# First layer's mixture of experts: every expert on every token, replaced by token rows sorted by expert in 127 tiles

## The chip, the cores and the metric

The program runs on one core of one Trainium2 chip (trn2). The metric is the device time of one execution in microseconds (us), all four layers included.

## The reference

A four-layer network on 1,024 tokens (16 sequences of 64) of width 256. Each layer does cross-attention to a context of 1,601 rows, self-attention, and a feed-forward part, each added to x. Only the feed-forward part of the first layer is changed. It is a mixture of 64 experts, of which each token uses 8, and one shared expert:

```
def _mlp(x, gw, uw, dw):
    return jax.nn.silu(x @ gw.T) * (x @ uw.T) @ dw.T
x = hidden_states.reshape(B * S, H)              # 1024 x 256, after a layer norm
rw = _route(x, gate_w, gate_bias)                # 1024 x 64, 8 nonzero weights in a row
expert_out = jax.vmap(lambda gw_, uw_, dw_: _mlp(x, gw_, uw_, dw_))(Wg, Wu, Wd)   # hidden width 176
routed = jnp.einsum('eth,te->th', expert_out, rw)
shared = _mlp(x, Sg, Su, Sd)                     # hidden width 352
out = (routed + shared).reshape(B, S, H)
```

All is float32. `_route` takes, for each token, the 4 best of 8 groups of experts and the 8 best experts in these.

## The kernel before

The program is a chain of stages. A stage (`stage`) gives each engine its own list of instructions, with semaphores between them, and ends with all engines meeting (line 44). Of the stages only these matter here.

`cross_attention` of layer 0 loads the context in pieces of 800.5 KB from SyncE's queue (line 440), two batches ahead.

`refresh` (tag nf0) adds the output of self-attention to x and makes the normed rows, turned into `net.xnT` (features on partitions, tokens along the row).

`route_groups` makes the routing weights `score` (tokens on partitions, 8 tiles of 64) on VectorE, a chain in which each step waits for the one before. Line 1390 is its last step. TensorE then turns them (line 1341), and VectorE copies them to `rwT` (line 1393).

`gated_experts` computes every expert on all 1,024 tokens. The hidden rows of all experts stand in 91 tiles of 128 (3 of the shared expert, 88 of the 64 routed ones), each with its gate, up and down weights (`e_w`, 384 KB). A tile is done in two units of 512 tokens. Each product is written as three float32r products of high and low parts (`split_product`, line 1458), so a unit has 18 matmuls of 512 columns: 6 for gate, 6 for up, 6 for down. ScalarE and VectorE split the weights and the hidden values into those parts. The down products of all 182 units are summed in the accumulators of PSUM. At the end the sum is turned and added to x (line 1529). The next stage, `refresh` nx1, begins with line 283 on VectorE.

`top1_experts`, the third layer's mixture (14 experts, 1 for each token), already works on sorted rows. It counts the tokens of each expert, gives each its place in 21 tiles of 128 rows, scatters the rows to `x_rows` in HBM by 8 indirect transfers of GpSimd (line 1638; 128 rows of 1 KB each), loads them back (line 1766), and takes each tile with its expert's weights (1,154 KB, line 1629, six slots): 2 transposes (line 1652), 8 matmuls of 128 columns (line 1664), 4 matmuls of 256 columns (line 1674), all plain float32. The trace has two records for each plain float32 matmul and one for each transpose. Each tile's output goes to `y_rows` (line 1625). When all are there, 8 indirect transfers (line 1642) bring the rows back into token order and line 1755 adds them.

## Time and profile before

| what | value |
|---|---|
| median of 3 runs | 4831.44 us (4830.58 to 4834.53) |
| the profiled execution: time, span | 4833.99 us, 4832.2 us |
| TensorE busy | 4280.3 us, 89% of the span |
| VectorE, ScalarE, GpSimd busy | 2477.3, 1964.5, 556.7 us |
| mean granted TensorE clock | 0.937 of 2.4 GHz |
| routing and experts of layer 0 | 919.5 to 1713.0 us of the span |
| moved by DMA | 223.20 MB, 46 GB/s over the span |

The busy shares are means over stages that differ. For this change the place to read is the stretch between line 1390 and the next stage's line 283. In the listing of instructions in order of time, a row gives start, duration, engine, line, operation, what it writes and reads, the count of instructions merged into the row, and in brackets how long the engine was idle before it and who ended that. A merged row's duration runs from its first start to its last end.

### The profile page before, as it was taken

The numbers are of one execution on the slowest core, as the hardware profiler recorded it, in microseconds if no ns is written. First come the engines' busy times: TensorE is split into PE (matmuls) and PEld (weight loads), VectorE is DVE, ScalarE is ACT, GpSimd is POOL, SyncE is SP. The second block draws the span as 40 slices with busy tenths as digits, with TensorE's granted clock in tenths as the row PEclk, the third lists the DMA queues.
The fourth block names the chain that finished last, engine by engine and source line by source line (L and its number), as shares of the span: only waits on it lengthen the run. The fifth ranks groups of instructions, "written<-read, shape, count | busy, mean of one in ns | idle before, by whom it ended". The sixth has DMA issues, their size and how long they took to land. (4 is left out here: it accounts for less than half of the span.)

```text
span 4832.2 us, 144528 instructions
## 1 busy us (share of the span) xinstructions
PE 4280.3 (89%) x65816; PEld 3416.8 (71%) x65816; DVE 2477.3 (51%) x4205; ACT 1964.5 (41%) x3848; POOL 556.7 (12%) x264
## 2 busy tenths in 40 slices
PE   7999996599999979999987689999973769999988
PEld 5877774488888858888863557787752648888865
DVE  4555553556666655555535535555534145555532
ACT  3545442233333334444532235454532234444431
POOL 1111111000000011111104001111102011111100
PEclk9999998599999989999988799999986889999988
DMA  2111100021111111111103011111110721111100
GB/s 70 43 37 40 39 23 17 19 80 48 48 50 50 46 56 38 41 42 38 38 24 84 19 41 41 43 37 43 37 19 10 283 67 38 45 38 38 38 10 31
DMA packets 89805, 223.20 MB, mean 46 GB/s; under 512 B 28880, under 2 KB 52576, under 8 KB 86480
## 3 DMA queue, kind: packets, MB, share of 16 engines
q1 hardware_dynamic: 85696, 209.13, 13.7%
q8 instruction: 521, 8.54, 0.7%
q10 hardware_dynamic: 2736, 2.75, 0.2%
q0 software_dynamic: 768, 2.10, 0.1%
q14 instruction: 84, 0.69, 0.1%
HBM read 196.23 MB, written 9.32 MB: 43 GB/s over the span
## 5 line engine op out<-in xcount | busy, mean ns | idle before, releaser
L647 DVE TENSOR_REDUCE x_pm<-banks 128x4 f32<-128x1536 f32 (+2 forms) x512 | 935.6, 1827 | 690.2 <-PE banks L548 690.2
L749 ACT ACTIVATE x_pl<-banks 128x384 f32<-128x384 f32 x1536 | 628.8, 497 | 710.2 <-PE banks L531 710.2
L473 POOL TENSOR_TENSOR x_cl<-xnT,x_ch 128x1601 fp32r<-128x1601 f32 x116 | 386.1, 3328 | 2176.7 <-ACT x_ch L764 2176.7
L754 ACT ACTIVATE x_kT<-banks,x_bk 128x384 f32<-128x384 f32 (+2 forms) x512 | 305.5, 597 | 537.4 <-PE banks L559 537.4
L571 PE MATMUL banks<-x_wh,x_ch 128*128 128x256 f32 (+1 forms) x1664 | 489.9, 294 | 0.0
L531 PE MATMUL banks<-x_q,x_kT 32*128 32x128 f32 x13312 | 483.0, 276 | 3.1 <-issue 2.9
L548 PE MATMUL banks<-x_kT,x_q 32*128 32x384 f32 (+2 forms) x4096 | 458.5, 512 | 14.0 <-DVE x_v L679 9.0
L571 PE MATMUL banks<-x_wh,x_cl 128*128 128x256 f32 (+1 forms) x1664 | 468.6, 282 | 0.0
L571 PE MATMUL banks<-x_wl,x_ch 128*128 128x256 f32 (+1 forms) x1664 | 466.9, 281 | 0.0
L559 PE MATMUL banks<-x_ch,x_wh 128*128 128x384 f32 (+2 forms) x1024 | 410.4, 401 | 44.2 <-DVE x_cl L730 43.1
L531 PEld LDWEIGHTS banks<-x_q,x_kT 32*128 32x128 f32 x13312 | 436.5, 185 | 7.0 <-issue 4.4
L679 DVE TENSOR_TENSOR x_v<-banks,x_bv 128x256 f32<-128x256 f32 (+1 forms) x832 | 316.8, 419 | 196.3 <-PE banks L571 196.3
L559 PEld LDWEIGHTS banks<-x_ch,x_wh 128*128 128x128 f32 x1024 | 194.2, 190 | 292.4 <-ACT x_pl L749 210.3
L749 ACT ACTIVATE x_pe<-banks 128x512 f32<-128x512 f32 x512 | 264.4, 602 | 292.5 <-PE banks L531 292.5
L580 PE MATMUL banks<-x_pl,x_v 128*32 128x64 f32 x18432 | 325.2, 222 | 49.4 <-issue 48.8
L559 PE MATMUL banks<-x_ch,x_wl 128*128 128x384 f32 (+2 forms) x1024 | 358.1, 350 | 0.0
L559 PE MATMUL banks<-x_cl,x_wh 128*128 128x384 f32 (+2 forms) x1024 | 357.8, 349 | 0.2 <-issue 0.2
L580 PEld LDWEIGHTS banks<-x_pl,x_v 128*32 128x32 f32 x18432 | 289.9, 112 | 54.6 <-issue 54.0
L571 PEld LDWEIGHTS banks<-x_wh,x_ch 128*128 128x128 f32 (+1 forms) x1664 | 307.9, 185 | 6.7
L571 PEld LDWEIGHTS banks<-x_wh,x_cl 128*128 128x128 f32 (+1 forms) x1664 | 308.1, 185 | 0.2
L571 PEld LDWEIGHTS banks<-x_wl,x_ch 128*128 128x128 f32 (+1 forms) x1664 | 307.4, 185 | 0.0
L666 DVE TENSOR_SCALAR x_num<-banks,parity 128x64 f32<-128x64 f32 x128 | 36.3, 284 | 523.3 <-PE banks L580 523.3
(345 smaller groups left out, 6964.2 us busy)
## 6 DMA issues: line engine op xcount, KB each, us to landing
xnT<-in_ctxT SPq DMA_DIRECT2D x120, 800.5 KB, 4.4
e_w<-in_L_pack SPq DMA_DIRECT2D x91, 384.0 KB, 3.1
e_w<-in_L_pack SPq DMA_DIRECT2D x21, 1154.0 KB, 7.6
a_swap<-a_raw SPq DMA_DIRECT2D x64, 128.0 KB, 2.3
actT<-in_ctxT SPq DMA_DIRECT2D x8, 800.5 KB, 4.9
e_rw<-routed_rows SPq DMA_DIRECT2D x64, 64.0 KB, 2.9
x_rows<-e_zero SPq DMA_DIRECT2D x1, 2688.0 KB, 9.6
e_xt<-x_rows ACTq DMA_DIRECT2D x3, 896.0 KB, 10.3
```

Of the source, the lines that this page charges most:

```text
L473: nc.gpsimd.tensor_tensor(cl[:, u, k, 0:CTX], staged(b, k), ch[:, u, k, 0:CTX], ALU.subtract).then_inc(low_done, 1)
L531: last = nc.tensor.matmul(sets[g % 2][j][0:n, (t - lo) * P:(t - lo + 1) * P], kT[r, c, t * P:t * P + n], qb[r, u, c], start=False, stop=Tr ...
L548: last = nc.tensor.matmul(into[j][:, 0:hi - lo], qb[r, u, c], kT[r, c, lo:hi], start=not masked, stop=True, skip_group_check=masked)
L559: last = nc.tensor.matmul(bank[:, 0:hi - lo], w[:, 0, k, c * P:(c + 1) * P], x[:, u, k, lo:hi], start=(k == n == 0), stop=(k == KC - 1 and ...
L571: last = nc.tensor.matmul(bank[0:w, (t - lo) * D:(t - lo + 1) * D], x[:, u, k, t * P:t * P + w], y[:, 1, k, :], start=(k == m == 0), stop= ...
L580: last = nc.tensor.matmul(bank[32 * j:32 * j + 32, e * S:(e + 1) * S], v[0:w, u, t, at:at + 32], probabilities(c, j, t, t + 1)[0:w, 0, e * ...
L647: nc.vector.tensor_reduce(pm[:, c, :, g], src[:, :, 0:hi - lo], AX.X, ALU.max).then_inc(max_done, 1)
L666: nc.vector.tensor_scalar(num[:, c], src, own, None, ALU.mult).then_inc(o_taken, 1)
L679: ins = nc.vector.tensor_tensor(heads, bank[0:w, (t - lo) * D:(t - lo + 1) * D].rearrange("p (h e f) -> p h e f", e=2, f=16), bvb[0:w].rea ...
L749: nc.scalar.activation(probabilities(c, j, lo, hi).rearrange("p t q -> p (t q)"), mine[j][:, 0:(hi - lo) * P], ACT.Exp).then_inc(exp_done, 1)
L754: nc.scalar.activation(kT[:, c, lo:hi], mine[1 if g == 0 and inside(b if c else b - 1) else 0][:, 0:hi - lo], ACT.Identity, bias=col[:, c: ...
```

## The change

`gated_experts` goes, with its high and low parts, and `routed_experts` comes in its place. The 8 x 1,024 pairs of token and expert are sorted by expert into 127 tiles of 128 rows (each expert begins a new tile, and 127 is the most that can be needed; all 127 are always computed). A tile takes its expert's weights in two transfers whose address comes from a register: gate and up, 128 rows of 2,816 bytes (360,448 bytes), and down, 88 rows of 2,048 bytes (180,224 bytes). Five slots hold them. The shared expert is 16 units on tokens in their own order, with weights that are loaded once. A unit has plain float32 matmuls: 2 of 352 columns for gate and up, 2 transposes of the hidden values, 2 matmuls of 256 columns for down; a routed one has 2 transposes of its rows besides. The rows are scattered by 64 indirect transfers and fetched back by 64, each of 128 rows of 1 KB. Sorted rows are loaded 8 tiles at a time (1,024 KB) and outputs stored 4 tiles at a time (512 KB). The HBM buffer of the sorted rows is cleared in 8 transfers of up to 2 MB during layer 0's cross-attention. `route_groups` no longer turns the weights. The diff, cut to its core:

```diff
+                if clear is not None and b < CLEARS:
+                    rows = clear[b * CLEAR_TILES * P:min(b * CLEAR_TILES + CLEAR_TILES, ROUTED_TILES) * P, :]
+                    rows = rows.rearrange("(j p) n -> p j n", p=P)
+                    sp.dma_start(rows, spread(net.zero[:].unsqueeze(1), (P, rows.shape[1], D))).then_inc(net.cleared, 16)
...
-def gated_experts(net, tag, packed, rwT, rw_rows):
...
+def routed_experts(net, tag, xn, score, mask, x_rows, y_rows):
...
+    E, K = 64, 8
+    GU, HID = 352, 88
+    WIDTH = KC * GU + 2 * D
+    SLOTS = 5
+    LOAD, X_RING = 8, 3
+    STORE, Y_RING = 4, 2
+    RING = 16
+    SHARED = 2 * TILES
+    UNITS = SHARED + ROUTED_TILES
+    LOADS = -(-ROUTED_TILES // LOAD)
+    STORES = -(-ROUTED_TILES // STORE)
...
+        def weights(n):
+            return ws[:, n % 2] if n < SHARED else w[:, (n - SHARED) % SLOTS]
...
 
         @block.sync
         def _(sp):
+            def load_rows(n):
+                tiles = tiles_of(n, LOAD)
+                rows = x_rows[tiles.start * P:tiles.stop * P, :].rearrange("(j p) n -> p j n", p=P)
+                sp.dma_start(xt[:, n % X_RING, 0:len(tiles)], rows).then_inc(x_in[n % X_RING], 16)
+            def load_weights(j):
+                e = sp.value_load(owner_i[0:1, j:j + 1], min_val=0, max_val=E - 1)
+                slot_w = w[:, j % SLOTS]
+                sp.dma_start(slot_w[:, 0:KC * GU], d["L0_pack"][bass.ds(e, 1)].rearrange("o p n -> p (o n)")).then_inc(w_in[j % SLOTS], 16)
+                sp.dma_start(slot_w[0:HID, KC * GU:], d["L0_down"][bass.ds(e, 1)].rearrange("o p n -> p (o n)")).then_inc(w_in[j % SLOTS], 16)
+            sp.dma_start(before[:], d["before"]).then_inc(const_in, 16)
+            sp.dma_start(const[:], d["sort_rows"]).then_inc(const_in, 16)
+            sp.dma_start(ws[:], d["L0_shared"].rearrange("s p n -> p s n")).then_inc(shared_in, 16)
+            sp.wait_ge(tiles_known, 1)
+            for j in range(SLOTS):
+                load_weights(j)
+            sp.wait_ge(scattered, 16 * TILES * K)
+            for n in range(X_RING):
+                load_rows(n)
+            for j in range(ROUTED_TILES):
+                sp.wait_ge(y_ready, j + 1)
+                if j + SLOTS < ROUTED_TILES:
+                    load_weights(j + SLOTS)
+                if j % LOAD == 0 and j and j // LOAD + X_RING - 1 < LOADS:
+                    load_rows(j // LOAD + X_RING - 1)
+                n = j // STORE
+                tiles = tiles_of(n, STORE)
+                if j == tiles.stop - 1:
+                    rows = y_rows[tiles.start * P:tiles.stop * P, :].rearrange("(j p) n -> p j n", p=P)
+                    sp.dma_start(rows, y[:, n % Y_RING, 0:len(tiles)]).then_inc(stored[n % Y_RING], 16)
+            for s in range(Y_RING):
+                sp.wait_ge(stored[s], 16 * ((STORES - s + 1) // Y_RING))
+        @block.gpsimd
+        def _(pool):
+            pool.wait_ge(net.cleared, 16 * CLEARS)
+            pool.wait_ge(slots_known, 1)
+            for n in range(TILES * K):
+                pool.indirect_dma_start(x_rows, bass.IndirectOffsetOnAxis(ap=slot_i[:, n:n + 1], axis=0), xn[:, n // K, :],
+                                        None).then_inc(scattered, 16)
+            for s in range(Y_RING):
+                pool.wait_ge(stored[s], 16 * ((STORES - s + 1) // Y_RING))
+            for n in range(TILES * K):
+                if n >= RING:
+                    pool.wait_ge(added, n - RING + 1)
+                pool.indirect_dma_start(yt[:, n % RING, :], None, y_rows,
+                                        bass.IndirectOffsetOnAxis(ap=slot_i[:, n:n + 1], axis=0)).then_inc(back[n % RING], 16)
...
+            def turn(n):
+                j = n - SHARED
+                load = j // LOAD
+                pe.wait_ge(x_in[load % X_RING], 16 * (load // X_RING + 1))
+                if j >= 2:
+                    pe.wait_ge(xT_ready, j - 1)
+                for c in range(KC):
+                    last = nc.tensor.transpose(x_ps[j % 2][:, c * P:(c + 1) * P], xt[:, load % X_RING, j % LOAD, c * P:(c + 1) * P],
+                                               net.ident[:])
+                last.then_inc(turned, 1)
+            def gate_up(n):
+                j = n - SHARED
+                if j >= 0:
+                    pe.wait_ge(w_in[j % SLOTS], 32 * (j // SLOTS + 1))
+                    pe.wait_ge(xT_ready, j + 1)
+                if n >= 2:
+                    pe.wait_ge(h_ready, n - 1)
+                for k in range(KC):
+                    x = net.xnT[:, k, (n // 2) * P:(n // 2 + 1) * P] if j < 0 else xT[:, j % 2, k]
+                    last = nc.tensor.matmul(gu_ps[n % 2][:, 0:GU], x, weights(n)[:, k * GU:(k + 1) * GU], start=(k == 0),
+                                            stop=(k == KC - 1))
+                last.then_inc(gu_full, 1)
+            def turn_hidden(n):
+                pe.wait_ge(h_ready, n + 1)
+                if n >= 2:
+                    pe.wait_ge(hT_ready, n - 1)
+                for i in range(2):
+                    last = nc.tensor.transpose(h_ps[n % 2][0:HID, i * P:(i + 1) * P], h[:, n % 2, i * HID:(i + 1) * HID], net.ident[:])
+                last.then_inc(h_turned, 1)
...
             def down(n):
+                o = output(n)
+                first, final = n >= SHARED or n % 2 == 0, n >= SHARED or n % 2 == 1
+                pe.wait_ge(hT_ready, n + 1)
+                if first and 2 <= o:
+                    if o - 2 < TILES:
+                        pe.wait_ge(shared_added, o - 1)
+                    else:
+                        pe.wait_ge(y_ready, o - 1 - TILES)
+                for i in range(2):
+                    at = KC * GU + i * D
+                    last = nc.tensor.matmul(y_ps[o % 2][:, 0:D], hT[:, n % 2, i], weights(n)[0:HID, at:at + D],
+                                            start=(first and i == 0), stop=(final and i == 1))
                 last.then_inc(down_done, 1)
...
+            pe.wait_ge(const_in, 32)
+            flat = mask[:].rearrange("p t e -> p (t e)")
+            nc.tensor.matmul(cum, before[:], flat, start=True, stop=True)
+            nc.tensor.matmul(count, net.ones[:], flat, start=True, stop=True).then_inc(counted, 1)
+            pe.wait_ge(owner_ready, 1)
+            nc.tensor.matmul(count[0:1, 0:P], owner[:], net.ident[:], start=True, stop=True).then_inc(owner_turned, 1)
+            pe.wait_ge(shared_in, 16)
+            for n in range(-3, UNITS):
+                if n + 3 == SHARED:
+                    pe.wait_ge(slots_known, 1)
+                    pe.wait_ge(tiles_known, 1)
+                if SHARED <= n + 3 < UNITS:
+                    turn(n + 3)
+                if 0 <= n + 2 < UNITS:
+                    gate_up(n + 2)
+                if 0 <= n + 1 < UNITS:
+                    turn_hidden(n + 1)
+                if n >= 0:
+                    down(n)
...
+            for t in range(TILES):
+                link(nc.vector.tensor_tensor(pre[:, t + 1], pre[:, t], count[:, t * E:(t + 1) * E], ALU.add))
...
+            def take_rows(n):
+                j = n - SHARED
+                dve.wait_ge(turned, j + 1)
+                if j >= 2:
+                    dve.wait_ge(gu_full, n - 1)
+                nc.vector.tensor_copy(xT[:, j % 2], x_ps[j % 2][:, 0:D].rearrange("p (c n) -> p c n", c=KC)).then_inc(xT_ready, 1)
+            def multiply(n):
+                dve.wait_ge(silu_done, n + 1)
+                if n >= 2:
+                    dve.wait_ge(h_turned, n - 1)
+                nc.vector.tensor_tensor(h[:, n % 2], g[:, n % 2], gu_ps[n % 2][:, 2 * HID:GU], ALU.mult).then_inc(h_ready, 1)
+            def take_output(n):
+                o = output(n)
+                dve.wait_ge(down_done, n + 1)
+                if n < SHARED:
+                    nc.vector.tensor_tensor(net.x[:, o], net.x[:, o], y_ps[o % 2][:, 0:D], ALU.add).then_inc(shared_added, 1)
+                    return
+                j = n - SHARED
+                s = j // STORE
+                if s >= Y_RING:
+                    dve.wait_ge(stored[s % Y_RING], 16 * (s // Y_RING))
+                nc.vector.tensor_copy(y[:, s % Y_RING, j % STORE], y_ps[o % 2][:, 0:D]).then_inc(y_ready, 1)
...
+            for n in range(-3, UNITS):
+                if SHARED <= n + 3 < UNITS:
+                    if n + 3 == SHARED:
+                        for t in range(TILES):
+                            find_weights(t)
+                    take_rows(n + 3)
+                if 0 <= n + 2 < UNITS:
+                    multiply(n + 2)
+                if n >= 0 and (n >= SHARED or n % 2):
+                    take_output(n)
...
+            for n in range(TILES * K):
+                t, k = n // K, n % K
+                dve.wait_ge(back[n % RING], 16 * (n // RING + 1))
+                if k:
+                    dve.wait_ge(added, n)
+                nc.vector.scalar_tensor_tensor(net.x[:, t, :], yt[:, n % RING, :], weight[:, t, k:k + 1], net.x[:, t, :], ALU.mult,
+                                               ALU.add).then_inc(added, 1)
...
+            def silu(n):
+                act.wait_ge(gu_full, n + 1)
+                if n >= 2:
+                    act.wait_ge(h_ready, n - 1)
+                nc.scalar.activation(g[:, n % 2], gu_ps[n % 2][:, 0:2 * HID], ACT.Silu).then_inc(silu_done, 1)
+            def take_hidden(n):
+                act.wait_ge(h_turned, n + 1)
+                if n >= 2:
+                    act.wait_ge(down_done, n - 1)
+                nc.scalar.activation(hT[:, n % 2].rearrange("p i n -> p (i n)"), h_ps[n % 2][0:HID, 0:2 * P], ACT.Copy).then_inc(hT_ready, 1)
+            for n in range(-3, UNITS):
+                if 0 <= n + 2 < UNITS:
+                    silu(n + 2)
+                if 0 <= n + 1 < UNITS:
+                    take_hidden(n + 1)
...
+ROUTED_TILES = (TOK * 8 + 64 * (P - 1)) // P
+CLEAR_TILES = 16
+CLEARS = -(-ROUTED_TILES // CLEAR_TILES)
...
+    o["L0_pack"], o["L0_down"] = (np.ascontiguousarray(m) for m in (routed[:, :, :704], routed[:, :88, 704:]))
```

`find_weights`, not shown, is three VectorE instructions of 512 elements for each of 8 token tiles. Between `need` and the first unit VectorE does some 25 further short steps on 64 to 512 elements, chained as those of `route_groups` are.

## Rows read from the trace of the kernel before

**Rows 1.** The page, busy time by engine.

```profile
PE 4280.3 (89%) x65816; PEld 3416.8 (71%) x65816; DVE 2477.3 (51%) x4205; ACT 1964.5 (41%) x3848; POOL 556.7 (12%) x264
```

**Rows 2.** Busy time in a stretch of `gated_experts`: length, engines, granted clock, DMA share, GB/s.

```profile
1300.00:1500.00 200.00, 200.00 (x884) 165.62 (x883) 125.50 (x172) 75.84 (x123) 0.00 (x0) 1.00 0.16 48
```

**Rows 3.** In order of time: both edges of the stretch that changes.

```profile
950.26 0.43 DVE L1390 TENSOR_SCALAR r_score<-r_score 128x512 f32<-128x512 f32 x1
...
954.88 0.80 SPq L1441 DMA_DIRECT2D e_w<-in_L_pack  x2
...
1713.05 0.43 DVE L283 BATCH_NORM_STATS2 nx_stats<-x_tok 128x6 f32<-128x256 f32 x1 [1.09 <-PEq L44]
```

**Rows 4.** In order of time: chained VectorE steps of `route_groups`.

```profile
939.89 2.04 DVE L1299 TENSOR_TENSOR r_eq<-r_eq,r_tri 128x64 f32<-128x64 f32 x8
...
942.69 0.69 DVE L1302 TENSOR_REDUCE r_rank<-r_gt 128x64 f32<-128x512 f32 x1
```

**Rows 5.** In order of time: one tile of `top1_experts` on TensorE.

```profile
3801.27 0.38 PE L1652 MATMUL banks<-ident,e_xt 128*128 128x128 f32 x2
...
3801.49 1.95 PE L1664 MATMUL banks<-e_xT,e_w 128*128 128x128 f32 x16
...
3803.28 1.89 PE L1674 MATMUL banks<-e_w,e_h 128*128 128x256 f32 x8
...
3805.01 0.38 PE L1652 MATMUL banks<-ident,e_xt 128*128 128x128 f32 x2
```

**Rows 6.** In order of time: first and last of 8 scatters.

```profile
3760.18 0.17 DVE L1735 CAST e_sloti<-e_slot 128x8 int32<-128x8 f32 x1
...
3761.25 1.21 POOL L1638 DMA_INDIRECT x_rows<-nf_xn,e_sloti  x1 [16.61 <-DVE e_sloti L1735]
...
3770.38 0.96 POOL L1638 DMA_INDIRECT x_rows<-nf_xn,e_sloti  x1 [0.31 <-issue]
```

**Rows 7.** In order of time: last output, first and last of 8 gathers, last addition.

```profile
3866.46 0.42 DVE L1751 TENSOR_TENSOR e_y<-banks,e_w 128x256 f32<-128x256 f32 x1 [1.30 <-PE banks L1674]
3868.88 0.97 POOL L1642 DMA_INDIRECT e_yt<-y_rows,e_sloti  x1 [97.54 <-DMA y_rows<-e_y]
...
3877.69 0.95 POOL L1642 DMA_INDIRECT e_yt<-y_rows,e_sloti  x1 [0.31 <-issue]
...
3880.50 0.48 DVE L1755 SCALAR_TENSOR_TENSOR x_tok<-e_yt,e_weight,x_tok 128x256 f32<-128x256 f32 x1 [0.78 <-DMA e_yt<-y_rows,e_sloti]
```

**Rows 8.** In order of time: SyncE's queue in `top1_experts`, six weight loads, later a steady tile.

```profile
3760.20 6.43 SPq L1629 DMA_DIRECT2D e_w<-in_L_pack  x6
...
3798.19 0.33 SPq L1625 DMA_DIRECT2D y_rows<-e_y  x1
3799.27 0.34 SPq L1629 DMA_DIRECT2D e_w<-in_L_pack  x1
```

**Rows 9.** Transfers by what they move: count, KB each, median us from issue to landing.

```profile
e_w<-in_L_pack SPq DMA_DIRECT2D x91, 384.0 KB, 3.1
...
a_w<-in_L_q SPq DMA_DIRECT2D x1, 1024.0 KB, 5.0
a_w<-in_L_k SPq DMA_DIRECT2D x1, 1024.0 KB, 7.9
...
e_yt<-y_rows,e_sloti POOLq DMA_INDIRECT x8, 2.8
```

**Rows 10.** In order of time: four context loads of layer 0.

```profile
67.29 62.77 SPq L440 DMA_DIRECT2D xnT<-in_ctxT  x4
```

**Rows 11.** Busy time in stretches of 4 and 2 us where weights, then sorted rows, are loaded.

```profile
3774.00:3778.00 4.00, 0.00 (x0) 0.00 (x0) 0.00 (x0) 0.00 (x0) 0.00 (x0) 0.50 1.02 427
...
3787.00:3789.00 2.00, 2.00 (x11) 2.00 (x11) 0.00 (x0) 0.00 (x0) 0.00 (x0) 0.50 1.11 350
```

**Rows 12.** Busy time around line 252 of `refresh` na0, granted clock third from last.

```profile
760.00:764.00 4.00, 0.48 (x3) 0.35 (x3) 1.36 (x3) 0.05 (x1) 0.03 (x1) 0.80 0.01 4
764.00:768.00 4.00, 4.00 (x10) 3.15 (x11) 1.26 (x4) 1.73 (x3) 4.00 (x6) 0.50 0.01 2
768.00:770.00 2.00, 2.00 (x8) 1.64 (x7) 1.62 (x8) 0.29 (x1) 1.55 (x3) 0.69 0.00 0
```

More of the change, by code:

```diff
@@ L1302, in rank_below, with route_groups @@
     link(nc.vector.tensor_reduce(rank, gt.rearrange("p t i j -> p (t i) j"), AX.X, ALU.add))
-def route_groups(net, tag, rwT):
+def route_groups(net, tag, score, left):
     nc, d = net.nc, net.dram
     E, G, K = 64, 8, 8
-    with ExitStack() as mem, stage(nc, "w_in logits sig chain rw_ready turned ones_set") as (
-            block, w_in, logits, sig, chain, rw_ready, turned, ones_set):
+    with ExitStack() as mem, stage(nc, "w_in logits sig chain rw_ready") as (
+            block, w_in, logits, sig, chain, rw_ready):
         w = net.sb(tag + "_gw", [P, KC, E], ctx=mem)
@@ L1454, in _ @@
         @block.tensor
         def _(pe):
-            def split_product(out, u, at, right, start, stop):
-                for m, (a, b) in enumerate(((wh, 0), (wl, 0), (wh, 1))):
-                    last = nc.tensor.matmul(out, a[:, u, at:at + P], right[b], start=start and m == 0,
-                                            stop=stop and m == 2, skip_group_check=not start and not stop)
-                return last
-            def down(n):
-                u, half = n // 2 % 2, n % 2
-                pe.wait_ge(h_lo, n + 1)
-                for c in range(KC):
-                    last = split_product(acc[c][half], u, o_d + c * P, (hh[:, n % 2], hl[:, n % 2]), n < 2, n >= UNITS - 2)
-                last.then_inc(down_done, 1)
@@ L1486, in _ @@
-            down(UNITS - 1)
-            for half in range(2):
-                pe.wait_ge(out_ready[half], 2)
-                for t in range(4 * half, 4 * half + 4):
-                    for c in range(KC):
-                        last = nc.tensor.transpose(net.ps[half][:, (t % 4) * D + c * P:(t % 4) * D + (c + 1) * P],
-                                                   out_sb[:, c, t * P:(t + 1) * P], net.ident[:])
-                last.then_inc(turned, 1)
+            def turn(n):
[8 more added lines that the diff above has]
+                last.then_inc(turned, 1)
@@ new lines, in _ @@
+            dve.wait_ge(const_in, 32)
+            link(nc.vector.tensor_tensor(steps[:], spread(pre[:, TILES].unsqueeze(2), (P, E, 8)),
+                                         spread(edges.unsqueeze(1), (P, E, 8)), ALU.is_gt))
+            link(nc.vector.tensor_reduce(need[:], steps[:], AX.X, ALU.add))
+            link(nc.vector.tensor_copy(sums[:, 0, E:], need[:]))
+            for s in range(6):
+                a, b = sums[:, s % 2], sums[:, 1 - s % 2]
+                link(nc.vector.tensor_tensor(b[:, E:], a[:, E:], a[:, E - (1 << s):2 * E - (1 << s)], ALU.add))
@@ L1533, in _ @@
+            dve.wait_ge(added, TILES * K)
         @block.scalar
         def _(act):
-            def split_high(tile):
-                u = tile % 2
-                act.wait_ge(w_in[u], 16 * (tile // 2 + 1))
-                nc.scalar.activation(wh[:, u], w[:, u], ACT.Copy).then_inc(w_hi, 1)
-            for half in range(2):
-                tok = slice(half * HALF, (half + 1) * HALF)
-                nc.scalar.activation(xh[:, :, tok], net.xnT[:, :, tok], ACT.Copy).then_inc(x_hi, 1)
-            split_high(0)
```

243 lines of the change are left out of this document (99 added, 144 removed).

## The prediction

> **What bounds the kernel now.** I read the page first: TensorE is busy for 89% of the span [rows 1]. A share over all stages does not price a change in one, so I went to the order of time at the edges of the stretch that changes [rows 3]: the routing weights are ready at 950.7 us (950.26 + 0.43) and the next stage's first VectorE step starts at 1713.05. These 762.4 us are what is replaced. A window in the middle [rows 2] shows TensorE busy for all of 200 us at the full clock with 884 matmul records, 0.226 us each. A unit has 18, so it takes 4.07 us, and 182 units take 741 us. DMA is at a share of 0.16 and VectorE at 0.63, so nothing but TensorE sets the pace, and what counts is how much time the new stage's TensorE, its transfers and its serial parts need.
>
> **TensorE per sorted tile.** `top1_experts` has the same kinds of instruction at the full clock [rows 5]. Two transposes start at 3801.27 and the next group at 3801.49: 0.22 us. Sixteen records of 128 columns take 1.79 us (to 3803.28), 0.112 each. Eight records of 256 columns take 1.73 us (to 3805.01), 0.216 each. A record thus costs about 0.004 us beside its columns, and one of 352 columns comes to 0.297. A sorted tile has four of these for gate and up (1.19 us), four of 256 for down (0.86) and two pairs of transposes (0.44): 2.49 us. 127 tiles are 316 us. Three units of the shared expert are unfinished when the first sorted rows are awaited (the loop turns rows three units ahead): one gate/up, two hidden turns, three downs, 1.19 + 0.44 + 2.6 = 4.2 us.
>
> **The serial part in front.** I keep to the clock of the span.
> - `route_groups` no longer turns and copies the weights. With a stage change of 1.1 us (the idle time in the last row of [rows 3]) the new stage issues its first transfer at 951.8, where before it was 954.9 [rows 3].
> - The constants land some 3.1 us later, as 384 KB do [rows 9]: 955.
> - Two count matmuls of 512 columns, four records, at half clock (four times 0.112, doubled, each): 3.5 us, 958.5.
> - The VectorE chain to the slots: some 20 short steps of 0.255 us (2.04 over 8), five on 512 elements at 0.72 (0.69 with a small gap) [rows 4], and eight maxima at 0.14 or so, estimated between those: 9.8 us, 968.3. The first scatter starts 1.07 us after its slots' step starts [rows 6]: 969.2.
> - 64 scatters. Eight took 9.13 us from first start to last start [rows 6], 1.30 each, so 63 intervals are 82 us: 1051.2. The last lands 2.8 us later, as a gather does [rows 9], and the first load of sorted rows (1,024 KB) takes 5.0 us [rows 9] and 0.3 of waking: 1059.3.
>
> Under these 90 us lie the shared expert's 16 units (2.27 us each, 36 us, and a few more at half clock), the three steps of `find_weights` per token tile (24 steps of 0.7, 17 us) and the first five weight loads (6 loads took 6.4 us to issue [rows 8]). They cost nothing, for the scatters last longer than all of them.
>
> **The tail.** After the last down: 0.42 us of copy and 2.0 us until the first gather [rows 7], and 0.8 for a last store three times the size: 3.2 us. 64 gathers at 1.26 us (8.81 over 7) and 3.3 us from the last one's start to the end of the last addition (3880.50 + 0.48) [rows 7]: 82.6 us. VectorE's additions stay hidden, 0.48 in each 1.26. Stage change 1.1 us.
>
> **The sum without stalls.** 1059.3 + 316.2 + 4.2 + 2.6 (TensorE comes from idleness and runs about 5 us at half clock, as after the gap in [rows 12]) + 3.2 + 82.6 + 1.1 = 1469.2. Against 1713.05 that is 243.8 us less. The profiled execution took 4833.99 us, of which 4832.2 are span, so 4590.2; it stands 2.5 us above the median shown, which makes 4588.
>
> **Other engines in the loop.** VectorE has two copies of 256 elements and a product of 176 per tile, about 0.42 + 0.42 + 0.33, ScalarE about 0.7: below 2.49. SyncE loads a value, issues two weight transfers, and a store every fourth and a row load every eighth tile. One load with its value takes 1.22 us (6.43 less 0.34, over 5) [rows 8]. The second transfer lies between 0.45 (a plain issue with its gap) and 1.22. I take 0.5; with stores and row loads 1.9 us per tile, at most 2.6.
>
> **The eight clears.** 2 MB each at 350 GB/s [rows 11] are 6 us of transfer, behind a context load. These loads come 20.8 us apart (62.77 less the issue, over 3) [rows 10], and DMA is mostly idle there, so each clear is over before the next load. Nothing; were every clear to delay a load that something waits for, up to 6 us each, 48 in all.
>
> **The transfers, where I expect the stalls.** Bytes per tile: weights 541 KB, output 131 KB, sorted rows 131 KB. With 9.2 KB rows the trace shows 427 GB/s, with 1 KB rows 350 [rows 11]. I take 380 for the weights and 350 for the rest: 1.42 + 0.37 + 0.37 = 2.2 us (bounds 1.9 and 2.3), below 2.49, so the mean rate does. The timing is tighter. The load for tile j+5 is released by tile j's output copy, 0.5 us after its down, and gate/up of j+5 comes two tiles and one pair of transposes after that down: 4.98 + 0.22 - 0.5 = 4.7 us. It needs 0.75 us until the issue (3798.52 to 3799.27) [rows 8], 3.1 us for 384 KB [rows 9] and 0.4 for the other 147 KB, 4.3 in all with the second issue. The slack is 0.35 us. Loads queue in order: of two loads of 1,024 KB issued 0.45 us apart the second lands 2.9 us later by its own issue, 3.35 in all [rows 9]. So a load of sorted rows holds the queue for 3.0 to 3.35 us, say 3.2, and a store of 512 KB for 1.5. The weights of the next tile are issued 2.49 us after those before, and find 1.42 + 3.2 - 2.49 = 2.1 us in front of them, and 0.4 from the store just before (1.42 + 1.5 - 2.49). Less the slack that is 2.2 us of TensorE stall at each of the 13 row loads in the loop: 29 us. Stores by themselves give 0.1 each, 1 or 2 us. In a busy queue every landing will be a little later; it goes round a loop of five tiles, so 0.3 us more is 0.06 per tile, 7 us. Together 37: **4588 + 37 = 4625 us**.
>
> **A rule on the 88 rows.** The Trainium skill, "DMA: Bandwidth & Descriptors", section on why a DMA increments its semaphore by 16, says that a transfer is spread over the largest number of engines up to 16 that divides its slowest dimension; for 88 rows that is 11. No transfer of this trace shows it. It is the second rival below.
>
> **The rivals.**
> 1. All transfers covered. For it: the mean need is 2.2 of 2.49 us, and in `top1_experts` a greater one never stalled TensorE. Against it: there six slots gave several times the lead. 4588, to 4600. Chance 0.15.
> 2. Down weights on 11 of the 16 DMA engines. These then move 55,296 bytes per tile (8 rows each of 2,816, 2,048, 1,024 and 1,024), at 380/16 GB/s 2.33 us, at 350/16 2.53, which is just over 2.49. The weights take 1.64 us, the slack falls to 0.1, a row load costs 2.9 us (13 times, 38), a store 0.5 (16 times, 8), and landings as above or a little worse 10: 4588 + 56 = 4644, to 4660. Chance 0.22.
> 3. The clock. After 4 us with TensorE busy for 0.48 it ran at 0.50, which is 1.2 GHz, until about 769 [rows 12]. If each of the 13 stalls brings that, half of 5 us is lost each time: 34 us more, 4660, with rival 2 4680. Against it: that gap followed a stretch with TensorE busy 0.48 of 4 us, mine follow 15 us of full work. Chance 0.13.
> 4. SyncE: with 1.22 us for the second transfer it needs 2.6 us per tile. The load's way also grows by 0.7. 127 times 0.11 and the stalls: 4640 to 4660. Chance 0.05.
> 5. Slower than before: the indirect transfers. The trace has only 8 in a row. If a queue of them holds no more than eight and each further one waits for an earlier one to land and be taken up, the interval is no longer 1.3 us. 112 of the 128 are beyond the eighth, and 206 us of forecast gain divided by them is 1.84, so the side changes at an interval of 3.1 us. At 4 us the kernel takes 4930. For it: nothing in the trace but that it ends at eight. Against it: landings of 2.8 us are longer than the interval, so at least two are in flight without a pause. Chance 0.05.
> 6. The forecast, 4600 to 4640: 0.40.
>
> **How the numbers follow.** The forecast is 4625. The range goes from 4586, with all covered, to 4700, which takes in rivals 2, 3 and 4, and 2 with 3 and the upper bounds of the loads; what is left out is rival 5 and worse queues than these, some 0.1. About 0.2% (10 us) is what a measurement can tell from no change. All cases but rival 5 are faster: 0.94. The same, 0.01: an interval of the indirect transfers just at 3.1. Slower 0.05.
>
> **What the profile after would show.** Right: records of 352 columns 0.30 us apart; 127 tiles in 350 to 360 us, with TensorE waiting for `w_in` (weights) once in eight tiles for about 2 us, one tile after each row load; two runs of 64 indirect transfers of 80 us with TensorE idle, 52 us or so in the first; layer 0's cross-attention unchanged. Wrong: waits for weights at every tile (rival 2, or a slower queue), the granted clock under 1 in the loop (3), SyncE issuing without waiting (4), intervals of POOL over 1.3 us (5), or a steady 2.49 us (1).

## The result, and the profile after

Changed kernel: 4763.06 us median of 4 runs (4757.26 to 4770.7). Kernel before, beside it: 4832.98 us. The ratio is 0.9854, 95% interval 0.9837 to 0.9871: faster by some 70 us, where I had forecast 4625 us and a range of 4586 to 4700. The same kernel run again later (`a_again`) gave 0.985. The direction was right; of the 206 us of gain that were forecast, some 70 came.

The page of the changed kernel, busy time by engine, answers to [rows 1]:

```profile
PE 3955.9 (83%) x64206; PEld 3096.3 (65%) x64206; DVE 2213.9 (47%) x4094; ACT 1766.6 (37%) x3675; POOL 679.0 (14%) x392
```

TensorE lost 324 us of work, the span only 77. The instructions in order of time, at the places of [rows 3], [rows 6] and [rows 7]:

```profile
984.68 0.33 SPq L1469 DMA_DIRECT2D e_before<-in_before  x1
...
1105.45 0.68 DVE L1641 TENSOR_TENSOR e_eq<-e_spot,e_slot 128x512 f32<-128x512 f32 x1
...
1558.70 0.98 POOL L1504 DMA_INDIRECT e_yt<-routed_y,e_sloti  x1 [476.61 <-DMA routed_y<-e_y]
...
1640.35 0.48 DVE L1663 SCALAR_TENSOR_TENSOR x_tok<-e_yt,e_weight,x_tok 128x256 f32<-128x256 f32 x1 [0.78 <-DMA e_yt<-routed_y,e_sloti]
1644.87 0.43 DVE L286 BATCH_NORM_STATS2 nx_stats<-x_tok 128x6 f32<-128x256 f32 x1 [4.04 <-PEq L40]
```

With the stalls, the forecast put the next stage at 1469.2 + 37 = 1506.2; it starts at 1644.87, 138.7 later. Place by place:

| term | forecast | measured | late by |
|---|---|---|---|
| stage's first transfer | 951.8 | 984.7 | 32.9 |
| from there to the first sorted turn | 107.5 | 121.0 | 13.5 |
| first sorted turn to its gate/up | 0.2 | 16.6 | 16.4 |
| 127 tiles, first gate/up to the last down's end | 359.8 | 432.5 | 72.7 |
| tail, gathers, stage change | 86.9 | 90.1 | 3.2 |

Three places make nearly all of it: the clears (priced at nothing), the shared expert and `find_weights` beside the scatters (priced at nothing, 13.5 + 16.4 us), and the loop (its stalls priced too low). In the loop the waits of TensorE, from 1122 to 1545 us, are:

```profile
PE banks L1529 <- DMA e_w<-in_L_down: 69.1, 41, 6.0
PE banks L1529 <- issue: 13.7, 1, 13.7
```

69 us in 41 waits for weights, where I had 37 in all. The second row is the first sorted tile waiting for VectorE's `find_weights`. A load of sorted rows (in short, a row load) and what it does, in order of time:

```profile
1184.51 0.39 SPq L1461 DMA_DIRECT2D e_xt<-routed_x  x1
...
1185.84 0.34 SPq L1466 DMA_DIRECT2D e_w<-in_L_pack  x1
...
1187.60 1.45 PE L1529 MATMUL banks<-e_w,e_xT 128*128 128x352 f32 x4 [0.74 <-DMA e_w<-in_L_down]
...
1195.60 2.71 PE L1529 MATMUL banks<-e_w,e_xT 128*128 128x352 f32 x4 [5.25 <-DMA e_w<-in_L_down]
```

And the same place as busy time (third from last: granted clock), answering to [rows 2] and [rows 12]:

```profile
1194.00:1200.00 6.00, 4.40 (x10) 2.97 (x11) 0.34 (x1) 0.70 (x2) 0.00 (x0) 0.52 0.56 179
...
1422.00:1522.00 100.00, 85.19 (x356) 59.88 (x355) 32.75 (x89) 17.73 (x58) 0.00 (x0) 0.91 0.72 221
```

The mechanism of the forecast is there. The tile whose weights were issued just ahead of the row load waits 0.74 us, and the tile whose weights were issued behind it (at 1185.84) waits 5.25: 6.0 us here, where I had 2.2. Over the 13 row loads of the loop these pairs of waits add up to 61.6 of the 69 us, 4.7 us for each. The landing events of the trace show that a transfer does not land at one moment: the 16 parts of this row load land from 1190.2 to 1193.0, those of the weights behind it from 1191.2 to 1195.56, and the matmuls start at 1195.60, with the last part. After the long wait the clock is granted at half, 1.2 GHz, for some 5 us: the tile's four records of 352 columns take 2.71 us instead of 1.35. A tile without a wait takes 2.49 us, as priced.

The clears, around the first one. TensorE in order of time, then the DMA queues in 92 to 96 us (packets, MB, share of 16 engines):

```profile
92.56 0.58 PE L587 MATMUL banks<-x_pe,x_v 128*32 128x64 f32 x25
95.96 0.33 PE L587 MATMUL banks<-x_pe,x_v 128*32 128x64 f32 x4 [2.82 <-issue]
```

```profile
q1 hardware_dynamic: 1478, 1.51, 106.8%
q8 instruction: 1, 0.02, 1.5%
```

TensorE stops for 2.8 us in the middle of a group of 32 matmuls, where the program has no wait, while the clear holds all DMA engines and one 16 KB packet of instructions is under way among its packets. From 96 to 102 us the clock is at half. In the traces of the changed kernel, of `a_again` and of `e2` (below) I count 30 gaps over 1.2 us in TensorE's work between 60 and 430 us, and each of the 30 has such a packet in it or ending at most 0.2 us before it. The packet itself takes no longer than in quiet stretches (0.96 us here), so that it was late because it stood behind the clear is inferred.

Last, the shared expert's units beside the scatters, ScalarE in order of time:

```profile
1008.78 0.32 ACT L1673 ACTIVATE e_g<-banks 128x176 f32<-128x176 f32 x1 [1.67 <-issue]
...
1060.42 0.32 ACT L1673 ACTIVATE e_g<-banks 128x176 f32<-128x176 f32 x1 [22.02 <-DMA nx_bq<-in_L_xattn_bq]
...
1088.43 0.32 ACT L1673 ACTIVATE e_g<-banks 128x176 f32<-128x176 f32 x1 [22.02 <-DMA nx_bq<-in_L_xattn_bq]
```

Until 1012 us a unit takes 2.27 us, as forecast. Then four units take 77 us, until some 5 us after the scatters are through; the transfer named as releaser was over long before. Each time it is a result of TensorE that reaches ScalarE or VectorE late (up to 17.5 us behind the recorded end), while what ScalarE and VectorE hand on arrives at once.

### The profile page after: what moved, and what is told of

The parts are those of the page before. It is cut to its first block and busy times, and to the rows that moved or that the text cites. A ratio compares the mean times of both kernels' runs of the same rounds, so it can differ in the third digit from the quotient of the medians.

```text
span 4755.4 us, 142721 instructions
## 1 busy us (share of the span) xinstructions
PE 3955.9 (83%) x64206; PEld 3096.3 (65%) x64206; DVE 2213.9 (47%) x4094; ACT 1766.6 (37%) x3675; POOL 679.0 (14%) x392
## 6 DMA issues: line engine op xcount, KB each, us to landing
routed_x<-zero SPq DMA_DIRECT2D x7, 2048.0 KB, 11.5
```

## The experiments

All start from the changed kernel. "Loop" is the time from the first sorted gate/up to the start of the last down record, "start" the stage's first transfer, "to tile 0" from there to the first sorted gate/up.

| run | ratio to before | start | to tile 0 | loop |
|---|---|---|---|---|
| changed kernel | 0.9854 | 984.7 | 137.6 | 432.1 |
| `a_again` | 0.985 | 979.6 | 139.5 | 434.1 |
| `e2_small_clears` | 0.9908 | 1005.9 | 135.8 | 437.9 |
| `e3_weights_first` | 0.9834 | 981.1 | 126.7 | 427.6 |
| `e4_scatter_after_units` | one run, 4756.81 us | 980.4 | 139.6 | 430.7 |
| `s8_slots8` | 0.9662 | 973.5 | 136.3 | 346.5 |
| `c_clears_in_self_attention` | 0.9717 | 945.1 | 111.0 | 435.8 |
| `l2_load2` | 0.9682 | 981.4 | 107.8 | 392.8 |
| `d8_down_128rows` | 0.9558 | 978.5 | 110.9 | 317.6 |
| `o8_one_transfer` | 0.9562 | 974.8 | 111.4 | 317.6 |
| `d5_down_128rows` | 0.9782 | 975.6 | 137.7 | 400.6 |
| `r5_down_80_and_8` | 0.9864 | 972.4 | 137.8 | 436.7 |
| `x8_down_96rows` | 0.9658 | 977.9 | 138.3 | 337.8 |
| `m_clears_between` | 1.0008 | 1047.3 | 139.3 | 438.7 |
| `n_clears_midway` | 0.9782 | 949.5 | 135.9 | 425.4 |
| `b_best` | 0.953 | 947.0 | 130.5 | 317.5 |

The intervals of the ratios are 0.001 to 0.0023 to either side; the other columns come from one profiled execution each. How far these scatter is seen in kernels that do not differ at the place: the start in 11 kernels with the eight clears of 2 MB is 972.4 to 984.7, the loop in 8 kernels that leave it alone 425.4 to 438.7. Four kernels (`c`, `l2`, `d8`, `o8`) ran together on one chip, and there "to tile 0" is 111.4 us or less; on three other chips, and in the first profile of the changed kernel, it is 126 or more. So kernels on different chips are compared by their columns, and by ratio only on the same chip.

**The clears.** Smaller ones first, one behind each context load:

```diff
-CLEAR_TILES = 16
+CLEAR_TILES = 5
                     load_context(b + 2, k)
+                    n = KC * b + k
+                    if clear is not None and n < CLEARS:
+                        rows = ...
```

> The same 16.3 MB of zeros, but in 26 transfers of 640 KB, one behind each context load, in place of 8 of 2 MB. Theory A (a 2 MB transfer fills the DMA engines for 6 us; the one instruction fetch that falls into it comes late, TensorE stands for 3 us in the middle of a group and then runs at half clock for 5 to 6 us, some 4 us lost at each clear): a 640 KB transfer lasts under 2 us, the fetch is hardly late, and the first transfer of the sorted stage comes at 952 to 960 us instead of 984.68, the whole kernel at 4732 to 4740 us. Rival B (every byte of a clear costs the same, by plain contention): no change within 5 us.

Neither came: the stage starts at 1005.9, some 28 us later than with the 2 MB clears. TensorE's unexplained waits in 60 to 420 us (total, times, longest) for this kernel, and then for the changed one (`a_again`):

```profile
PEld banks L588 <- issue: 32.3, 28, 3.8
PE banks L588 <- issue: 24.5, 14, 3.6
```

```profile
PEld banks L587 <- issue: 22.4, 23, 2.4
PE banks L587 <- issue: 15.9, 9, 2.3
```

The kernel before has 6.2 us in 5. The gaps have not gone. A clear right behind a context load is one burst with it. The size and the time from issue to landing of a clear in the changed kernel, in `e2`, and in `n_clears_midway` (below), where it lies alone:

```profile
routed_x<-zero SPq DMA_DIRECT2D x7, 2048.0 KB, 11.5
routed_x<-zero SPq DMA_DIRECT2D x25, 640.0 KB, 7.1
routed_x<-zero SPq DMA_DIRECT2D x25, 640.0 KB, 3.3
```

The extra time comes from their number. ScalarE takes up the 19th piece of context at 428.8 us in the kernel without clears in this stage (`c`, next), at 466.2 in the changed one, which has then done all eight of its clears, and at 468.0 in `e2`, which has done 17 of 26; the 29th piece at 645.7, 683.7 and 705.2. So a small clear behind a load costs 2.3 us and a large one 4.1 to 4.7, and there are three times as many. Moved out of the stage (in `attend_pairs`, one behind each of its eight steps):

```diff
+            if extra_bias == "alibi":
+                for n in range(CLEARS):
+                    sp.wait_ge(biased, n + 1)
+                    rows = net.to_clear[...]
+                    sp.dma_start(rows, spread(net.zero[:].unsqueeze(1), ...)).then_inc(net.cleared, 16)
```

> The eight clears of 2 MB issued in layer 0's self-attention instead, one for each of its eight pairs of batches, some 9 us apart, where VectorE sets the pace and TensorE issues a tenth of the instructions. Theory A (in the cross-attention a clear holds up an instruction fetch of TensorE and costs the clock): the cross-attention ends as in the kernel before, nothing waits in the self-attention, and the kernel gains 25 to 35 us on the changed one, a ratio to the kernel before of 0.978 to 0.980. Rival B (the clears cost the same wherever they lie): 0.985 as the changed kernel.

The start is at 945.1: the clears' whole cost is gone, 33 us against the mean of 978 of the eleven kernels that have them unchanged. (The forecast's 951.8 was itself 6.7 us late, and the first profile's 984.7 is the latest of the eleven.) The rest of its ratio, under the 0.978 expected, goes with the chip ("to tile 0"). To tell the burst from the count, the small clears were put between the loads, with `sp.wait_ge(s_full, CYCLES * b + 4 * k + 7)` ahead of each:

> The 26 clears of 640 KB again in the cross-attention, but issued midway between two context loads rather than right behind one, where they made the kernel 28 us slower than the 2 MB clears did. Theory A2 (a burst costs when it lasts longer than TensorE can go without its next instruction fetch, and a small clear right behind a context load made 26 long bursts): alone, each lasts 2 us, less than a context load's 2.3, and the sorted stage starts at 945 to 955 us. Rival B2 (each transfer of zeros in this stage costs 1 to 1.5 us wherever it lies): the stage starts at 985 us or later.

The slowest of all (4832.85 us, the time of the kernel before), so this run does not decide between the two; and it is not the clears that make it slow: SyncE stood in that wait when the next context load was due, and ScalarE waited for it:

```profile
ACT x_ch L773 <- DMA xnT<-in_ctxT: 51.6, 13, 5.4
```

TensorE's gaps in mid-group were gone. With `4 * k + 2` in place of `4 * k + 7`, so that SyncE is free again in time:

> The 26 clears of 640 KB once more, now behind the second and sixth of a batch's eight score groups, some 8 us after a context load is due, so that SyncE is free again before the next load is. In the run before, the wait stood until the seventh group, SyncE came late to every second context load (15 us late, ScalarE waited 4 us for each of 13), and the stage began at 1047 us; but TensorE's unexplained gaps in the middle of groups were gone. Theory A2 (length of the burst decides): no such gaps (under 7 us in 60 to 420 us, as in the kernel before, against 16 with 2 MB clears and 24 with small ones behind the loads), no late load, and the sorted stage starts at 943 to 957 us. Rival B2 (each transfer costs wherever it lies): 975 us or later.

```profile
PEld banks L589 <- issue: 11.7, 21, 1.8
...
PE banks L589 <- issue: 5.0, 5, 1.7
```

The start is at 949.5 and the gaps are those of the kernel before: the same bytes in as many transfers, where they lie alone, leave the start 4.4 us behind that of `c`, which is within the scatter of the starts. Rival B2 is out, and theory A2 has its numbers. What stays untested is whether it is the length of the burst or that a write stands right behind a load.

**The shared expert and `find_weights`.** All eight calls of `find_weights` ahead of VectorE's loop over the units:

> The 24 steps of find_weights moved ahead of VectorE's loop over the units. Theory: they stand exposed behind the shared expert's units (1105.4 to 1121.8 us), so moved under the scatters they cost nothing and the kernel gains 14 to 17 us, to about 4747. Rival: the shared expert's units start 17 us later, their stalls move with them, and the end of the stage stays where it is (0 to 3 us).

"To tile 0" falls by 11 to 13 us against the changed kernel and by 9 to 10 against `e2` and `s8` on the same chip: more than half of the 16.4, for the units' backlog then shows. The ratio is 0.002 lower, which lies within the two intervals. GpSimd made to wait for the units:

```diff
             pool.wait_ge(slots_known, 1)
+            pool.wait_ge(shared_added, TILES - 2)
```

> GpSimd waits for six of the eight additions of the shared expert before its first scatter, so that units and scatters no longer lie side by side. Theory C (running indirect scatters hold up TensorE's completions): the units run at 2.27 us each throughout, all but three are done within 36 us of the slots, also beside the first five weight loads; the kernel is 20 to 25 us slower than the changed one, since nothing is hidden. Rival D (the units are held up by the first five weight loads, which keep the DMA engines full, and what follows is their backlog): the units stall here as well, from some 10 us after the weight loads start.

One run only. Busy time from 1000 to 1020 us, with weight loads and no scatter:

```profile
1000.00:1020.00 20.00, 20.00 (x90) 14.79 (x89) 4.74 (x14) 5.39 (x18) 0.00 (x0) 1.00 0.38 110
```

Rival D is out: the units run at full pace beside the loads. The expected loss of 20 to 25 us did not come: tile 0 comes no later than in the changed kernel, since the hiding had failed there anyway. And on one chip four kernels show no hold-up at all; here `d8` with units, scatters and weight loads together, 997 to 1030 us:

```profile
997.00:1030.00 33.00, 29.25 (x130) 21.19 (x128) 10.90 (x26) 7.79 (x27) 25.07 (x27) 1.00 0.70 252
```

> The changed kernel once more, unaltered, as the control of this group. In its first profile, and in those of three kernels of the first group (small clears, find_weights first, eight slots), the shared expert's units were held up between the scatters; in the four kernels of the second group they were not, though nothing there touches this place. If that belongs to the kernel, the hold-up is seen here as well and find_weights starts 120 us behind the stage's first transfer; if it belongs to the chip or the execution, it can be absent, with find_weights 46 us behind the first transfer and a ratio to the kernel before near 0.979 in place of 0.985.

The unaltered kernel shows the hold-up again (139.5). By `e4` it needs running scatters, and it is absent in the four profiles from one chip and present in the other profiles with scatters beside the units. Why TensorE's results are late then, and why not there, stays open.

**The loop.** Three more slots, `SLOTS = 8`:

> Eight weight slots in place of five. Theory L (the stalls are bursts: the row loads and stores hold the queue for 3 us and the lead is only 4.7 us of time): with three more tiles of lead, 7.5 us, the waits for the weights go to under 10 us of 69, the granted clock in the loop to 0.98 or more, and the kernel to 4680 to 4700 us. Rival R (the DMA engines cannot carry a tile's bytes in 2.49 us, whether by bytes or because 88 rows use only some of the engines): the waits stay nearly as they are, 4745 to 4760 us.

The loop falls from about 432 to 346.5 us and the ratio to 0.9662 (4660.78 us, better than the 4680 expected), with the clock at 0.98; but 17.7 us of waits in 11 are left, not under 10. So both theories have a part: the lead was most of it, and rival R's rate is what remains (below). Then the row loads in small pieces, `LOAD, X_RING = 2, 9`:

> Five slots, the sorted rows loaded two tiles (256 KB) at a time instead of eight (1 MB). Theory L (the stalls come from the bursts, each row load holding the queue for 3 us against a lead of 4.7 us): most of the waits for weights go, from 69 to under 25 us, and the ratio is 0.972 to 0.977. Rival (the lead is too short for the weights' own way in a busy queue, bursts or not): the waits stay above 50 us and the ratio above 0.981.

Loop 392.8 with waits of 47.3 us in 57, longest 2.6: between what the theory (under 25) and the rival (over 50) had said; the ratio, 0.9682, is helped by the chip. Small pieces bring half of what eight slots bring (43 us against `c` on the same chip). The rest is not the bursts: five slots are short even for the weights' own way. For what remained, the down weights were padded:

```diff
-    (routed[:, :, :704], routed[:, :88, 704:])
+    (routed[:, :, :704], routed[:, :, 704:])
-                sp.dma_start(slot_w[0:HID, KC * GU:], d["L0_down"]...
+                sp.dma_start(slot_w[:, KC * GU:], d["L0_down"]...
```

> Eight slots, and the down weights fetched as 128 rows (40 of them zeros), still in a transfer of their own. If 88 rows keep only 11 of 16 DMA engines at work, the fullest engine carries the same bytes as before (8 rows), so nothing changes: within 5 us of the kernel with eight slots alone (ratio 0.9662). If bytes count, 82 KB more per tile at 289 GB/s are 0.28 us, 127 times: up to 36 us more, less what was slack, so 0.970 to 0.974.

> Eight slots, and a tile's weights in one transfer of 128 rows of 4,864 bytes, as the kernel before packs them: this part of the change undone. By bytes it carries as much as the kernel with 128 down rows, 0.970 to 0.974 of before; if longer rows run faster (427 against 350 GB/s for the longest and the 1 KB rows in the trace of before) it gets some of it back, 0.965 to 0.968; if the two transfers cost something of their own (the second issue, a second landing), it is faster than the kernel with eight slots, under 0.965.

Neither "nothing" nor "slower": with 15% more weight bytes the loop falls from 346.5 to 317.6 us, 127 tiles at 2.49, without a wait. With one transfer it is the same, but both run at TensorE's own pace, so a small difference between them would not show. Busy time from 1150 to 1350 us for eight slots with 88 rows, and with 128:

```profile
1150.00:1350.00 200.00, 185.42 (x866) 135.15 (x865) 78.98 (x218) 43.23 (x144) 0.00 (x0) 0.98 0.96 289
```

```profile
1150.00:1350.00 200.00, 200.00 (x965) 148.11 (x964) 87.64 (x240) 48.14 (x161) 0.00 (x0) 1.00 1.00 358
```

At a share of 0.96 the queue moves 289 GB/s, which is 301 for a full share; with 128 rows 358. A tile's 803 KB (weights 541, rows and output 262) take 2.67 us at 301 GB/s, more than TensorE's 2.49; the 885 KB with padding take 2.47 at 358. So the rate of the queue binds the kernel with 88 rows even with eight slots: 346.5 us over 127 tiles is 2.73. The DMA counts for the same stretch (under 512 B are the completions, the small packets that end a transfer):

```profile
DMA packets 36248, 57.84 MB, mean 289 GB/s; under 512 B 2369, under 2 KB 20719, under 8 KB 36230
```

```profile
DMA packets 44454, 71.66 MB, mean 358 GB/s; under 512 B 3069, under 2 KB 23796, under 8 KB 44433
```

The packets of 2 to 8 KB are the weights, 216 a tile in the first kernel and 256 in the second. That is 71.8 and 80.6 tiles, and 33.0 and 38.1 completions per tile. With 16 for the gate and up weights, 4 for a quarter of a store and 2 for an eighth of a row load, 11.0 and 16.1 are left for the down weights: a transfer of 88 rows does run on 11 engines. That is what the Trainium skill says ("DMA: Bandwidth & Descriptors", section "Why a DMA increments its semaphore by 16 and not by 1"), and the trace agrees. But by this rule the fullest engine carries 8 rows of the down weights either way, so the rule alone does not give the gain. Three more, first 128 rows with five slots:

> The changed kernel with five slots, and the down weights fetched as 128 rows. With 88 rows a tile leaves 33 small packets (completions) in the trace, with 128 rows 38, so a transfer of 88 rows runs on 11 engines. Theory E (the 11 engines are what binds, at a lower rate than 16 reach): the waits for weights fall from 69 us to under 45 and the loop of 432 us to 375 to 400. Rival L (the lead of five slots against bursts binds, the engines do not): with 15% more weight bytes the waits stay or grow, the loop takes 430 us or more.

Loop 400.6, waits 52.1 us in 37: the way of theory E, but just outside both of its bounds (400 and 45 us); rival L, which had the loop at 430 or more, is out. Per full share the queue moves some 330 GB/s here, so 128 rows alone do not give the 358 of eight slots:

```profile
1150.00:1350.00 200.00, 168.01 (x720) 118.38 (x721) 65.51 (x179) 36.60 (x120) 0.00 (x0) 0.94 0.81 269
```

Then `for lo, hi in ((0, 80), (80, HID))` around the down transfer:

> Five slots, the 88 down rows without padding but in two transfers, 80 rows (divisible by 16) and 8 rows: the bytes of the changed kernel on more engines, for one more issue of 0.35 to 0.5 us on SyncE. Theory E (engines): the fullest engine carries 7% less, the loop takes 370 to 400 us, as with 128 rows or a little better. If it is the third issue and landing that count instead, or bytes alone decide, the loop stays at 425 to 440 us.

```profile
DMA packets 29643, 45.83 MB, mean 229 GB/s; under 512 B 2586, under 2 KB 17493, under 8 KB 29628
```

Theory E fails: 46 completions per tile (2586 over 56.2), so 16 and 8 engines, fewer bytes on the fullest, and still 436.7 us and 76.2 us of waits. And 96 rows with eight slots:

> Eight slots, the down weights fetched as 96 rows: 96 is divisible by 16, so all 16 engines carry it, 6 rows each, and the bytes are only 3% over those of 88 rows. With eight slots the loop took 346.5 us with 88 rows and 317.6 with 128. Theory N (what matters is that all 16 engines share every transfer): as fast as 128 rows, 317 to 322 us. Theory P (what matters is that each engine's rows are the same ones in every transfer, eight for each, which holds for 128 rows and not for 96 or for 80 and 8): every packet stays slow, and the loop takes 335 us or more.

```profile
1150.00:1350.00 200.00, 192.42 (x905) 140.93 (x904) 82.32 (x227) 45.11 (x150) 0.00 (x0) 0.98 1.05 305
```

337.8 us, over the bound set for theory P: all 16 engines are at work, share 1.05, and move 305 GB/s, 290 for each full share against 358. So it is not the count of engines. What goes with the slow rate is seen in two more numbers of these traces. With eight slots and 88, 96 and 128 rows a packet of 2,816 bytes takes 149, 154 and 123 ns on average between 1150 and 1350 us, and the parts of one tile's weights land over 7.2, 5.0 and 2.7 us (medians from 1130 us on): the engines get out of step. Theory P fits all five kernels: dealt out in order over all 16 engines, only 128 rows would give each engine the same eight in every transfer. But no trace shows which rows an engine carries, and what collides was not seen, so this cause is argued and not shown.

**Together.** Clears in the self-attention, eight slots, one transfer of 128 rows, `find_weights` first:

> All that helped: the clears in the self-attention, eight slots, one transfer of 128 rows of 4,864 bytes, find_weights first. By the ledger: the sorted stage starts at 945 us, its loop takes 317 us, nothing else changes: 4605 less 33, some 4572 us, a ratio of 0.946 to 0.949. If the clears and the weights' gains overlap somewhere (the same clock, the same fetches), 0.950 to 0.956.

4598.92 us median, ratio 0.953 (0.9514 to 0.9546), 157 us faster than the changed kernel on the same chip. Start and loop are as expected. Against 4572 it misses 27 us, of which 19.5 are the hold-up beside the scatters (130.5 us to tile 0 against 111), which I had taken from the chip without it; that the ratio falls into the expected 0.950 to 0.956 for overlapping gains is luck.

## Why the prediction was right in direction and wrong in size

- **TensorE per sorted tile, 2.49 us:** right, wherever no transfer is late and the clock is full. The tail, 64 scatters and 64 gathers at 1.27 and 1.25 us, and the chain to the slots (16.6 us from the stage's first transfer to the first scatter, forecast 17.4): right. Rival 5 is out.
- **"Nothing; were every clear to delay a load ..., up to 6 us each":** failed. The cost was looked for at the context loads. What came late was TensorE itself, by all signs its instruction fetch, and then the clock was at half. Moving the clears shows the cost, 33 us (`c`, `n`); the fetch is inferred from the packet in every gap.
- **"They cost nothing, for the scatters last longer than all of them":** failed on all chips but one, where the 111 us to tile 0 are near the forecast's 107.7. Elsewhere units beside scatters are held up (13.5 us), and `find_weights`, which stands behind them in VectorE's order, is then bare (16.4 us). The sum of durations was right, the independence was not, and I had not read where in VectorE's order the 24 steps stand.
- **"1.42 + 0.37 + 0.37 = 2.2 us (bounds 1.9 and 2.3), below 2.49, so the mean rate does":** failed. It takes 2.67 us at the 301 GB/s that a full share moves with 88 rows (`s8`). The 350 GB/s of [rows 11] stood at a share of 1.11, so 315 for a full share, which I did not take into account; 427 at 1.02 was for rows of 9.2 KB.
- **"2.2 us of TensorE stall at each of the 13 row loads":** the mechanism was right, the size was not: 4.7 us at each, 61.6 in all where I had 29. A row load lands 6.7 to 8.9 us after its issue in the loop (5.0 in [rows 9]), and the next weights wait for their last part. Eight slots took 86 us out of the loop (`s8`), small row loads 43 (`l2` against `c`), 128 rows 33 (`d5` against `a_again`). These overlap.
- **Rival 3, the clock:** true beside the forecast's stalls. The loop is 432.5 - 322.8 = 110 us over the forecast's work without stalls; 69 us are waits, and of the other 40 some 30 are the clock (0.93 on average over 432 us), near the 34 of the rival. Ten or so are not accounted for.
- **Rival 2, 11 of 16 engines:** the spread is as the rule says, my sum by it (4644) is not: it took the fullest engine's bytes at the full rate.
- **The range:** it took in rivals 2 and 3 together (4680). With the loop alone as measured, 72.7 us over the forecast, the time would be 4698, still inside. What took it out are the two costs that stood at nothing with a named cover, 33 and 30 us; the bound of 48 us for the clears was written down and left out of the range's upper end.

## What to carry to other kernels

Price a transfer hidden beside a busy TensorE by the length of the burst that it makes with its neighbours; split it and place the pieces where they lie alone, or move it to a stage where TensorE issues little. Give a prefetch ring (the slots that are loaded ahead) a lead longer than the largest burst in its queue. Compare the bytes per tile with the rate at a full share, that is, divide a measured rate by its share. Where a queue is full and a transfer has fewer than 128 rows, try it padded to 128: here it paid, though the cause is open. When work is called hidden under other work, read each engine's order for what stands behind it.

## What the runs showed of the hardware that I had not expected

- A 2 MB write right behind an 800 KB load (11.5 us from issue to landing) goes with a stop of TensorE of 2 to 4 us in mid-group and a 16 KB instruction packet in or just before the gap; after the stop at 93 us the clock was at 1.2 GHz for 6 us. 640 KB alone (3.3 us) add nothing to the gaps of the kernel before.
- With eight slots, padding 88 rows to 128 raised the rate from 289 to 358 GB/s, and 96 rows gave 305; the parts of one tile's weights landed over 7.2, 2.7 and 5.0 us. With five slots 88 rows gave 229 to 234, 80 and 8 rows 229, 128 rows 269.
- While 64 indirect scatters run, a unit of 2.27 us takes up to 28 us on three chips and in the first profile, where TensorE's results reach the other engines up to 17.5 us late; on one more chip there is no delay.
